# First-layer softmax with exponentials two heads wide, its side work in a new slot table, and a new order of weight splitting and transfers around the second layer's attention

## The reference

```python
h = layernorm(x) * (1 + ca) + sa
x = x + ga * attention0(h)        # causal; scores = (q.k + q_rope.k_rope) / sqrt(40)
h = layernorm(x) * (1 + cb) + sb
x = x + gb * ffn0(h)              # 15 routed experts (top 3) and a shared one, all computed densely
h = layernorm(x) * (1 + ca1) + sa1
x = x + ga1 * attention1(h)       # not causal, grouped projections, scale 8 ** -0.5
h = layernorm(x) * (1 + cb1) + sb1
x = x + gb1 * ffn1(h)             # 8 experts, top 1, with a layernorm of its own
```

## Time and profile before

| | |
|---|---|
| runs | 982.16, 982.47, 984.56 us (median 982.47) |
| the profiled execution | 984.84 us, of which the span from first to last instruction is 983.1 us |
| busy share of the span | PE 81%, DVE 66%, ACT 53%, POOL 35% |
| layer 0's attention | about 61 to 318 us |
| dense experts | about 318 to 569 us |
| layer 1's attention | about 569 to 841 us |
| drain and expert blocks | 841 us to the end |

### The profile page before, as it was taken

The page is one execution under the profiler, slowest core; times in us unless marked ns, Lnnn a source line. Parts: engine busy times, 40 slices in busy tenths (PEclk is TensorE's granted clock), DMA queues, the critical chain, the costliest instruction groups (busy, mean ns, idle before and its releaser), DMA issues. The chain is left out here.

```text
span 983.1 us, 12967 instructions
## 1 busy us (share of the span) xinstructions
PE 792.4 (81%) x4212; PEld 497.0 (51%) x4212; DVE 649.1 (66%) x1290; ACT 524.2 (53%) x970; POOL 344.6 (35%) x389
## 2 busy tenths in 40 slices
PE   3547888988898889999989899789989888527850
PEld 2233444555454667787767544345344444227740
DVE  3135568676663777776768696488898876347853
ACT  1013454545556677776757456456656656217740
POOL 3413775543532000000005345653453542133425
PEclk9987999999999999999999979899999999659985
DMA  4251331102110490000002112210110200011013
GB/s 125 48 95 21 85 81 35 34 22 46 30 24 2 137 285 6 1 1 1 1 8 57 43 42 63 60 35 17 38 25 18 58 4 10 4 54 56 32 34 84
DMA packets 56414, 44.75 MB, mean 46 GB/s; under 512 B 6598, under 2 KB 47387, under 8 KB 56347
## 3 DMA queue, kind: packets, MB, share of 16 engines
q1 hardware_dynamic: 55323, 41.82, 16.8%
q0 software_dynamic: 1024, 2.10, 0.7%
HBM read 14.67 MB, written 14.55 MB: 30 GB/s over the span
## 5 line engine op out<-in xcount | busy, mean ns | idle before, releaser
L926 ACT ACTIVATE ring<-single 128x512 f32<-128x512 f32 (+3 forms) x512 | 253.1, 517 | 226.3 <-PE single L1176 218.8
L1554 DVE TENSOR_REDUCE mneg<-pair 128x2 f32<-128x1024 f32 (+3 forms) x256 | 258.5, 1022 | 87.7 <-PE pair L1160 33.2
L1176 PE MATMUL single<-q_op,k_op 104*128 104x512 f32 (+3 forms) x512 | 216.5, 443 | 17.8 <-ACT ring L926 9.2
L1156 PE MATMUL pair<-k_op,q_op 96*128 96x512 f32 (+3 forms) x512 | 172.1, 415 | 42.2 <-DVE mneg L1554 22.6
L786 POOL TENSOR_SCALAR k_op<-k_stk,cst 104x512 fp32r<-104x512 f32 x64 | 100.0, 1577 | 276.2 <-DMA k_stk<-hl 258.5
L1176 PEld LDWEIGHTS single<-q_op,k_op 122*128 122x128 f32 (+1 forms) x512 | 97.9, 197 | 98.6 <-ACT ring L926 72.6
L1156 PEld LDWEIGHTS pair<-k_op,q_op 120*128 120x128 f32 (+1 forms) x512 | 98.9, 207 | 86.8 <-DVE mneg L1554 44.8
L1192 PE MATMUL p_o<-ring,vaug 128*9 128x512 f32 (+3 forms) x1024 | 116.1, 526 | 1.0 <-ACT ring L926 0.9
L721 POOL TENSOR_SCALAR_AFFINE_SELECT ring<-ring 128x256 f32<-128x256 f32 x128 | 52.3, 408 | 149.4 <-ACT ring L926 149.2
L955 ACT ACTIVATE ring<-pair,cols 128x512 f32<-128x512 f32 x136 | 86.1, 685 | 33.8 <-PE pair L1236 27.5
L1600 DVE TENSOR_TENSOR ring<-ring,single 128x1024 f32<-128x1024 f32 x60 | 73.3, 1221 | 45.5 <-ACT ring L955 44.4
(11 more groups left out here) (294 smaller groups left out, 1306.4 us busy)
## 6 DMA issues: line engine op xcount, KB each, us to landing
xs<-zero SPq DMA_DIRECT2D x10, 1024.0 KB, 10.1
q_op<-hl SPq DMA_DIRECT2D x96, 64.0 KB, 2.0
stage<-in_L_ffn_W_dram SPq DMA_DIRECT2D x8, 512.0 KB, 4.5
stage<-in_L_ffn_rW_dram SPq DMA_DIRECT2D x6, 512.0 KB, 5.1
k_op<-hl SPq DMA_DIRECT2D x48, 64.0 KB
k_stk<-hl SPq DMA_DIRECT2D x48, 64.0 KB, 2.0
xb<-xs SPq DMA_DIRECT2D x15, 128.0 KB, 2.0
xs<-yb SPq DMA_DIRECT2D x15, 128.0 KB, 1.7
```

The costliest lines, as they stand in the source:

```text
L926: exp_done.by(act.activation(ring[:, n % 8, lo:T], singles[n % 2][:, lo:T], ACT.Exp), (L, n))
L1156: ins = pe.matmul(both[:, i, 0:hi], r32(qs[:, P * qt:P * (qt + 1)]), r32(ks[:, 0:hi]), start=i == 0 or L == 1 or qt >= 2, stop=L == 1)
L1176: st_full.by(pe.matmul(singles[n % 2][:, lo:T], r32(ks[:, P * kc:P * (kc + 1)]), r32(qs[:, lo:T]), start=True, stop=True), (L, n))
L1554: s_taken.by(dve.tensor_reduce(mneg[:, G % 2, 2 * p:2 * p + 2, qt], both[:, :, 0:hi], axis=AX.X, op=ALU.max, negate=True), (L, m))
```

## The change

Seven things, all in this diff:

1. Layer 0's exponentials: each `exp_unit` now computes two heads into a `pair` tensor (two PSUM banks), and ACT takes both in one instruction, so a quad has two such steps and not four. `pairs` and `singles` swap roles in layer 0.
2. Layer 0's `max_unit` now uses a `single` bank: two heads for the first two query blocks, one head for the other two, so a group has 12 units and not 8. They are spread over four quads: 4, 3, 3 and 2.
3. Layer 0's `TABLE` is spaced out; `values` of the quad before moves to the end of the quad; in row 0 the `P.*` parts come two quads later, and the norms of rows 1 to 3 are computed there together (`BATCH`), all three rows in each Newton step.
4. In layer 0 ACT and no longer DVE writes the normalised rows (`P.ne`, `T.ne`).
5. In layer 0 POOL's weight pieces and rotary copies are moved by a few half-quads.
6. In layer 1 POOL's eight weight pieces go two to each row (before: all in row 4), each behind a `mask`; `modulate` comes behind `mask(G + 4)` and `scatter` behind `mask(G + 6)`; the second half of each split is two instructions.
7. On SP, layer 0's `m_dma(0, G + 2)` is issued ahead of `rope_dma`; in layer 1 `head1_dma(G + 5)` comes ahead of `m_dma(1, G + 3)`, `head1_dma(G + 6)` ahead of `m_dma(1, G + 4)`, and the weight loads come last in each row.

The core of it (`T.ne`'s branch, semaphore lists, buffer placement and renamed bounds are left out):

```diff
+SCORES = [[(heads, qt) for p in (0, 2) for heads, qt in (((p, p + 1), 0), ((p, p + 1), 1), ((p,), 2), ((p + 1,), 2), ((p,), 3), ((p + 1,), 3))],
+          [((p, p + 1), qt) for p in (0, 2) for qt in range(NT)]]
+SU, NE = [len(SCORES[L]) for L in range(2)], [2, GH]
...
-        spread = (((-5, (0, 1, 2)), (-4, (3, 4, 5)), (-3, (6, 7))), ((-6, (0, 1)), (-5, (2, 3)), (-4, (4, 5)), (-3, (6, 7))))[L]
+        spread = (((-5, range(0, 4)), (-4, range(4, 7)), (-3, range(7, 10)), (-2, range(10, 12))),
+                  ((-6, (0, 1)), (-5, (2, 3)), (-4, (4, 5)), (-3, (6, 7))))[L]
...
-TABLE = [{(0, "b"): ["P.ns"], (0, "d"): ["T.ot3", "P.na"], (1, "b"): ["P.n1", "P.n2"], (1, "d"): ["T.on", "P.n3"],
-          (2, "b"): ["mt1", "P.ne"], (2, "d"): ["T.proj"], (3, "b"): ["P.ln1", "T.ns"], (3, "d"): ["P.rp", "T.na"],
-          (4, "b"): ["T.n1"], (4, "d"): ["P.rs", "T.n2"], (5, "b"): ["ot0", "T.n3"], (5, "d"): ["P.q"],
-          (6, "b"): ["mt2", "T.ne"], (6, "d"): ["P.k"], (7, "b"): ["P.v"], (7, "d"): ["T.ln2"],
-          (8, "b"): ["T.hin"], (8, "d"): ["T.lg"], (9, "b"): ["ot1"], (9, "d"): ["T.ex"], (10, "b"): ["mt3"],
-          (10, "d"): ["T.rt1"], (11, "b"): ["T.rt2"], (12, "b"): ["T.gt"], (13, "b"): ["ot2"], (14, "b"): ["P.mt0"]},
+TABLE = [{(0, "b"): ["P.ne"], (1, "b"): ["T.ot3"], (1, "d"): ["P.ln1"], (2, "b"): ["T.on"], (2, "d"): ["mt1"], (3, "b"): ["T.proj"],
+          (4, "b"): ["P.rp"], (4, "d"): ["P.q"], (5, "b"): ["ot0"], (5, "d"): ["P.rs"], (6, "b"): ["P.k", "T.ns"], (6, "d"): ["mt2"],
+          (7, "b"): ["T.na"], (7, "d"): ["P.v"], (8, "b"): ["T.n1"], (8, "d"): ["T.n2"], (9, "b"): ["ot1", "T.n3"], (9, "d"): ["T.ne"],
+          (10, "b"): ["T.ln2"], (10, "d"): ["mt3", "T.hin"], (11, "d"): ["T.lg"], (12, "b"): ["T.ex"], (12, "d"): ["T.rt1"],
+          (13, "b"): ["ot2"], (14, "b"): ["T.rt2"], (14, "d"): ["P.mt0"], (15, "b"): ["T.gt"]},
...
+BATCH = {(0, "b"): "B.s1", (0, "d"): "B.s2", (1, "b"): "B.s3", (1, "d"): "B.sd", (2, "b"): "B.n1"}
-WEIGHT_STEP = {at: n for n, at in enumerate([(0, k) for k in (*range(6, 16), *range(20, 24), *range(28, 32))]
+WEIGHT_STEP = {at: n for n, at in enumerate([(0, k) for k in (*range(6, 18), *range(22, 24), *range(28, 32))]
...
+    if a == 0:
+        later = [entry for entry in TABLE[0].get((q - 2, place), []) if entry[:2] == "P." and entry != "P.mt0"]
+        entries = [entry for entry in entries if entry[:2] != "P." or entry == "P.mt0"] + later
+        out += [(BATCH[q, place], 0)] if (q, place) in BATCH else []
...
-            pair = pairs[m % 2]
-            return pair[:, 0, :].rearrange("p (i k) -> p i k", i=2) if L == 0 and m % 4 < 2 else pair[:, :, :]
+            heads, qt = SCORES[L][m % SU[L]]
+            return pairs[m % 2][:, :, :] if L else singles[m % 2][:, :].rearrange("p (i k) -> p i k", i=len(heads))
...
                     expert0(4)
+                m_dma(0, G + 2)
                 if r < NB - 1:
                     rope_dma(r + 1)
                 if r == 0:
                     expert0(5)
-                m_dma(0, G + 2)
...
-                if r == 0:
-                    expert1(2)
-                    expert1(3)
                 m_dma(1, G + 2)
                 if r < NB - 1:
                     head1_dma(G + 4)
-                if r == 0:
-                    expert1(4)
-                    expert1(5)
+                    head1_dma(G + 5)
                 m_dma(1, G + 3)
-                if r == 0:
-                    expert1(6)
-                    expert1(7)
                 if r < NB - 1:
-                    head1_dma(G + 5)
+                    head1_dma(G + 6)
                     m_dma(1, G + 4)
-                    head1_dma(G + 6)
                     head1_dma(G + 7)
+                    expert1(2 * r + 2)
+                    expert1(2 * r + 3)
 
             blocks_of = xs.rearrange("(b p t) d -> p b (t d)", t=2, p=P)
             table_ready.wait_ge(sp, 0)
...
-                split1.by(pool.tensor_tensor(r32(lo), src, hi, ALU.subtract), n)
+                pool.tensor_tensor(r32(lo[:, 0:1, :]), src[:, 0:1, :], hi[:, 0:1, :], ALU.subtract)
+                split1.by(pool.tensor_tensor(r32(lo[:, 1:2, :]), src[:, 1:2, :], hi[:, 1:2, :], ALU.subtract), n)
...
-                    elif 16 <= k < 20 and r < NB - 1:
-                        rope_copy(4 * r + 4, k // 2 % 2, k % 2)
+                    elif 18 <= k < 22 and r < NB - 1:
+                        rope_copy(4 * r + 4, (k - 18) // 2, k % 2)
...
-                if s == NB:
-                    for n in range(0, 4):
-                        weights1(n)
-                else:
-                    modulate(s - 1)
                 if s < STAGES - 1:
                     mask(G + 4)
-                if s == NB:
-                    for n in range(4, 6):
-                        weights1(n)
+                if s > NB:
+                    modulate(s - 1)
+                weights1(2 * (s - NB))
                 if s < STAGES - 1:
                     mask(G + 5)
-                if s == NB:
-                    for n in range(6, len(PIECE1)):
-                        weights1(n)
-                else:
-                    scatter(s - 1)
+                weights1(2 * (s - NB) + 1)
                 if s < STAGES - 1:
                     mask(G + 6)
+                if s > NB:
+                    scatter(s - 1)
             modulate(STAGES - 1)
             scatter(STAGES - 1)
 
...
+                if name == "P.ne" and L == 0:
+                    normed.wait_ge(act, ("B.n1", L) if r else key)
+                    if r == 3:
+                        full.wait_ge(act, ("ln2", s - 3))
+                    apart(act)
+                    for t in range(NT):
+                        shift, scale = norm_of("P", s, t)
+                        ins = act.activation(xn[:, t, :], x[:, r, t, :], ACT.Identity, bias=shift, scale=scale)
+                    xn_ready.by(ins, key)
...
-                exp_done.by(act.activation(ring[:, n % 8, lo:T], singles[n % 2][:, lo:T], ACT.Exp), (L, n))
+                if L:
+                    ins = act.activation(ring[:, n % 8, :], singles[n % 2][:, :], ACT.Exp)
+                else:
+                    at = 2 * (n % 4)
+                    ins = act.activation(ring[:, at:at + 2, lo:T], pairs[n % 2][:, :, lo:T], ACT.Exp)
+                exp_done.by(ins, (L, n))
...
-                for i in range(2):
-                    qs, ks = operands(L, G, 2 * p + i, 24)
-                    ins = pe.matmul(both[:, i, 0:hi], r32(qs[:, P * qt:P * (qt + 1)]), r32(ks[:, 0:hi]), start=i == 0 or L == 1 or qt >= 2, stop=L == 1)
+                for i, j in enumerate(heads):
+                    qs, ks = operands(L, G, j, 24)
+                    ins = pe.matmul(both[:, i, 0:hi], r32(qs[:, P * qt:P * (qt + 1)]), r32(ks[:, 0:hi]), start=i == 0 or L == 1, stop=L == 1)
...
+                for k, j in enumerate((i,) if L else (2 * i, 2 * i + 1)):
+                    qs, ks = operands(L, G, j, 26)
+                    dst = singles[n % 2] if L else pairs[n % 2][:, k, :]
+                    ins = pe.matmul(dst[:, lo:T], r32(ks[:, P * kc:P * (kc + 1)]), r32(qs[:, lo:T]), start=True, stop=True)
+                st_full.by(ins, (L, n))
...
+                    if L == 0:
+                        exp_unit(L, Q, 0)
+                        for m in waiting[0:2]:
+                            max_unit(L, m)
+                        exp_unit(L, Q, 1)
+                        for name, b in beside_quad(s, q, "b"):
+                            part(name, b)
+                        for m in waiting[2:]:
+                            max_unit(L, m)
+                        if Q:
                             values(L, Q - 1)
...
+            def batch(what):
+
+                v, y, z = (nwtB[:, i, :] for i in range(3))
+                if what[0] == "s" and what[1] != "d":
+                    b = int(what[1])
+                    dve.wait_ge(loads[4], n_load[4])
+                    norm_stats("P", x[:, b, :, :])
+                    for t in range(NT):
+                        ins = dve.bn_aggr(mvB[:, NT * (b - 1) + t, :], stats["P"][:, t, :])
+                    step(ins)
+                elif what == "sd":
+                    step(dve.tensor_scalar(v, mvB[:, :, 1], EPS, None, ALU.add))
+                    step(dve.tensor_scalar(y.bitcast(I32), v.bitcast(I32), -0.5, float(0x5F3759DF), ALU.mult, ALU.add))
+                else:
+                    for i in range(3):
+                        newton_step(v, y, z)
+                    normed.by(dve.scalar_tensor_tensor(out=z, in0=y, scalar=-1.0, in1=mvB[:, :, 0], op0=ALU.mult, op1=ALU.mult), ("B.n1", 0))
 
```

153 lines of the change are left out of this document (90 added, 63 removed).

## The result

| | before | after |
|---|---|---|
| median | 982.32 us (4 runs, 979.23 to 984.56) | 997.25 us (4 runs, 994.60 to 1001.39) |
| ratio | | 1.0158, 95% interval 1.0107 to 1.0209 |
| the profiled execution | 984.84 us, span 983.1, granted clock 0.934 | 999.75 us, span 998.0, granted clock 0.916 |
| layer 0's attention, first exponential to last | 255.9 us | 264.9 us |
| layer 1's attention | 267.6 us | 273.6 us |

The change makes the kernel 1.6% slower; I had predicted 963 us and gave a slower result 5 in 100.

The account below looks back on a forecast made before the run. Layer 0's attention was taken as bound by PE's own work plus PE -> ACT -> PE round trips. Layer 0 -23 us and layer 1 +4 gave -19 from 984.8, so 966; the median, 2.4 lower, 963 us, range 943 to 977.

Parts of the forecast that it names:

- -22 - 4 - 4 + 4 + 2 + 1 = -23 us: Layer 0's sum: exponentials -22, DVE's relief -4, spread parts -4, late transpositions +4, POOL in row 0 +2, start +1.
- I take most of the 25.4 us as removed: 22 us.: Layer 0: two-head exponentials remove PE's weight-load waits for ACT, 22 us of 25.4, bounds 6 and 25 us.
- the terms for the table and the norms: Layer 0: spread parts -4 us, late transpositions +4 (0 to +9), norms' relief of DVE -4 (between -10 and +8).
- Rival 2: Chance 0.15, about 975 us: waits move to DVE and the maxima's transfer; layer 0 gives 12 us, layer 1 costs 4.
- Of 4.4 + 3.3 us I take back 4: Layer 0: spreading parts shortens waits for DVE's half of a part in the shared bank, 4 us (0 to 8).
- +2 us (0 to +4): Layer 0, row 0: POOL's cuts and pieces limit the gain, rotary rows come two quads later; cost 2 us.
- hidden behind an ACT that is idle 103 us: Layer 0: ACT's four Identity instructions per norm, 1.8 us per norm, hidden by ACT's idle time.
- the hole: Layer 1, row 4: PE's 6.13 us wait for group 5's mask goes, with slow matmuls behind it: -8 us.
- the new wait: Layer 1, rows 5 and 6: `T.hs` waits 7.5 us for `modulate`, PE 6.1 us each; +12 us (+6 to +15).
- The masks' places: Layer 1: earlier masks should remove PE's remaining 6.6 us of waits; credited -4 us, DVE being nearly full.
- POOL beside DVE: Layer 1: some five of nine Newton steps a row lengthened by 0.58 us beside busy POOL; +4 us (0 to +8).
- Slower: Rival, chance 0.05, about 990 us: layer 0's single-bank maxima make PE wait 0.68 us at every third of 180 units.

Follow-up runs that it names:

- q_after_rs: l1_modulate_first with `P.q` and `P.rs` exchanged in layer 0's table, so ACT's half of `q` comes one quad later: 982.87 us, ratio 0.9981.
- filled_hole: l1_modulate_first with 20 bf16 matmuls of 512 columns put into row 0's hole of 5.8 us before group 4's first maxima unit: 988.50 us, ratio 1.0043.
- l1_modulate_first: The changed kernel with `modulate` ahead of `mask(G + 4)` in layer 1, as before the change: 987.37 us, ratio 1.0032.
- pieces_in_idle_time: Kernel before plus wide exponentials and layer 1's new order (modulate first), all eight weight pieces moved behind row 4's `mask(G + 3)`: 973.56 us, ratio 0.9897.
- row0_rows_one_quad_later: q_after_rs with only row 0's `P.ne` moved from (2, "b") to (3, "b"): 973.00 us, ratio 0.9845.

## Why the prediction was wrong

**The sum's form.** "-22 - 4 - 4 + 4 + 2 + 1 = -23 us" adds terms that are not independent. The waits that I named moved the way I said: for ACT 25.4 to 8.8 us, for the maxima 17.1 to 10.7, that for the transfer up from 3.8 to 5.6 us at the matmuls (I had added 4). PE's visible idle time stayed at 28 or 29 us.

**The step that failed.** "I take most of the 25.4 us as removed: 22 us." The value depends on what PE meets next: 0 under the old table, where the transposition waits for the maxima, 25 to 33 us under the new one. The lower bound of 6 us, from the matmul rows, was no bound either. And the terms for the table and the norms, near nothing in the sum, cost 37 us in the trace with narrow exponentials (255.9 to 292.8) and 5 with wide ones (255.0 to 259.8). From the kernel before to the changed one, layer 0 thus goes -0.9 us by the exponentials, +4.8 by the table, and +5.1 between two executions of the same layer 0 at granted clocks of 0.93 and 0.90. Rival 2 had the mechanism (waits move to DVE and the transfer) for the old table; in the changed kernel it was right for the transfer only, since the wait for the maxima fell.

**The parts of the table.** "Of 4.4 + 3.3 us I take back 4": at the matmuls such waits for DVE's half went from 6.5 us to 5.1, two of 1.8 us for `q` among them, because I looked only at the distance to the part before it and not at what `q` waits for itself, the transfers that still read `hl`. q_after_rs shows it. This was the general omission: every part that moved earlier should have been followed to what it needs.

**Row 0.** "+2 us (0 to +4)" was +10. I had seen that the rotary rows come "close to group 4's first maxima" and had priced POOL's copies; the operands themselves, in SP's queue behind a wait of 5.9 us for these rows, six rotary transfers and two loads, cost PE 5.8 us. I did not follow SP's queue there. And I had costed ACT's normalised rows at nothing, "hidden behind an ACT that is idle 103 us": ACT is idle, but its stream is in order, and the exponentials stood behind a wait for the batch (2.81 us of PE).

**The clock.** It was no term of the sum. Layer 0 had 0.96 over its length before (20 us at the lower level) and 0.90 after (53 us): 33 us more, at 0.3 us each, are an estimated 10 us, the size of layer 0's whole loss of 9. By this estimate new waits and removed ones cancel without them. That the clock falls behind PE's idleness is shown in one place by filled_hole; why it falls behind one wait of a microsecond and not behind the next stays open.

**Layer 1** came out at +6 us for +4, partly by luck. Right were the hole (row 4 -8.7 us, predicted -8) and the new wait (`T.hs` 7.46 us for 7.5, PE 5.84 for 6.1). Two terms missed and nearly cancelled. The masks' places gave 9.1 us in the quads 2 of rows 5 to 7, where I had credited 4: waits of 6.6 us and a lower clock behind them had stood there. Quads 9 and 10 of rows 5 and 6 cost 22 us, where the two waits stood with 12 and POOL beside DVE with 4: behind the waits the clock was 0.55 to 0.79, which was in no term. That modulate causes the waits is shown by l1_modulate_first. The term "POOL beside DVE" was right in kind, and pieces_in_idle_time shows it larger than 4 us: 14 us in rows 5 to 7, lower clock included. The rule named for it in the prediction (the Trainium skill, SBUF — State Buffer, "Who interferes with whom") holds beside the weight pieces, the steps long and the reductions untouched. Beside the masks, which read SBUF too, it does not: there the two-input steps kept their 0.16 us (28 of 30), so the measurement decides, and my "busy throughout with a mask and two pieces" counted the mask wrongly.

**The chances.** Slower had 0.05 and one mechanism, the single banks, which was not the one in the changed kernel. Its condition was also mis-summed: waits at every fifth of 180 units are 36 x 0.68 = 24.6 us, 7.5 more than before, which does not turn a gain of 19 us; it takes about every third. The start, row 0, ACT's rows and the clock had each been taken at 2 us, 1 us or nothing.

## What to carry to other kernels

Where PE's visible idle time is 28 us, a wait of 25 us at its weight loads is not worth 22: first ask what PE meets next if it goes, and measure that change alone. When a part is moved earlier, follow it to what it waits for, on every queue, SP's too; when work is moved to an idle engine, ask what stands behind it in that engine's order. Count the lower clock behind a new wait as part of its price: here 0.3 us on average for each us at the lower level.

## What the hardware showed that I had not expected

- Stretches at the lower level stand behind waits of PE of only one or two us (row 2's quad 10 behind 0.84 and 1.06 us, at a clock of 0.60), and they stand in other places when something far ahead moves by a few us: in filled_hole mending one place did not lower the total.
- The same kernel's runs spread with it: row0_rows_one_quad_later from 963.0 us (clock 0.940) to 984.0 us (0.912), the kernel before from 978.0 to 993.3 over all comparisons.
- DVE's small steps beside POOL's weight pieces go up to 1.26 us for a copy of four columns, 0.16 us without, and splitting POOL's subtraction in two, as the change does, does not prevent it. Beside POOL's mask instructions two-input steps kept their 0.16 us in 28 of 30 cases.
